# A two-layer graph attention kernel on one core: the two transfers of each attention row move from SyncE's queue to ScalarE's

## The reference

```python
def gat(h, adj, W, a):                  # one layer, per graph
    Wh = h @ W
    e = (Wh @ a_left)[:, None] + (Wh @ a_right)[None, :]
    e = where(e > 0, e, 0.2 * e)
    attention = softmax(where(adj > 0, e, very_negative), axis=-1)
    return attention @ Wh

h = maximum(layernorm(x), 0)
x = x + elu(gat(h, adj, W0, a0))
h = maximum(layernorm(x), 0)
x = x + gat(h, adj, W1, a1)
```

## Time and profile before

| what | us |
|---|---|
| median of three timed runs (lowest, highest) | 301.15 (300.55, 301.64) |
| the profiled execution, its own time | 300.98 |
| its span (first to last instruction) | 299.0 |
| TensorE busy in it | 289.5 (97%) |
| VectorE busy | 259.1 (87%) |
| ScalarE busy | 190.8 (64%) |
| transfers of q1, SyncE's queue, as a share of 16 DMA engines' span | 73.3% |
| mean granted TensorE clock, of 1 | 0.989 |

### The profile page before, as it was taken

One profiled execution on the slowest core, in us unless ns is written; L12 is line 12 of the kernel. 1 busy time (PEld: TensorE's weight loads), 2 busy tenths in 40 slices (PEclk: granted clock), 3 DMA queues, 4 the chain that ended last, 5 costly groups with the idle time before them and its releaser, 6 DMA issues.

```text
span 299.0 us, 6658 instructions
## 1 busy us (share of the span) xinstructions
PE 289.5 (97%) x2541; PEld 287.7 (96%) x2541; DVE 259.1 (87%) x538; ACT 190.8 (64%) x489; POOL 82.5 (28%) x157
## 2 busy tenths in 40 slices
PE   7999997599999999999999999999999999999996
PEld 7999997599999999999999999999999999999996
DVE  4798794599898989989898998979798879879896
ACT  3387681768594968769496877748574764754410
POOL 2721704002507052340706134240705124000000
PEclk9999999599999999999999999999999999999999
DMA  7999996939779593949769395985959789682012
GB/s 231 415 406 410 407 404 183 412 156 375 301 271 411 161 412 144 405 173 347 287 200 414 78 390 195 343 352 192 384 196 360 284 293 398 179 328 110 35 72 70
DMA packets 26383, 83.59 MB, mean 280 GB/s; under 512 B 4976, under 2 KB 6128, under 8 KB 26352
## 3 DMA queue, kind: packets, MB, share of 16 engines
q1 hardware_dynamic: 25776, 82.78, 73.3%
q10 hardware_dynamic: 576, 0.39, 0.4%
HBM read 78.91 MB, written 4.25 MB: 278 GB/s over the span
## 4 chain that ended last, share of the span: by engine, by line
PE 92%; DMA 4%; ACT 1%; DVE 0%; issue 0%; POOL 0%; POOLq 0%
PE acc L905 70%; PE prj L844 10%; PE tp L783 5%; DMA r_rows<-sqr 3%; PE acc L920 2%; PE acc L775 2%; DMA row_by_node<-r_rows 1%; PE prj L847 1%; ACT row_r L417 1%; PE prj L816 1%; PE tp L852 1%; PE prj L920 1%; PE prj L905 1%; PE acc L825 1%; ACT wh L389 0%; ACT hT L375 0%
## 5 line engine op out<-in xcount | busy, mean ns | idle before, releaser
L905 PE MATMUL acc<-wh,pbuf 128*128 128x129 f32 x1968 | 227.8, 275 | 0.2
L905 PEld LDWEIGHTS acc<-wh,pbuf 128*128 128x128 f32 x1968 | 224.2, 192 | 0.5 <-ACT wh L359 0.3
L660 DVE SCALAR_TENSOR_TENSOR pbuf<-row_r,sqr,adj_sb 128x1024 f32<-128x1024 f32 x126 | 156.3, 1276 | 12.3 <-ACT row_r L417 12.3
L424 ACT ACTIVATE accs<-accs,rec 128x128 f32<-128x128 f32 x120 | 36.7, 389 | 43.7 <-DVE rec L679 43.7
L268 POOL TENSOR_TENSOR mean<-stats 128x8 f32<-128x8 f32 x14 | 11.6, 830 | 148.2 <-DVE stats L548 147.0
L369 ACT ACTIVATE xn<-x_sb,shift,rstd 128x128 f32<-128x128 f32 x120 | 47.7, 479 | 0.0
L417 ACT ACTIVATE row_r<-row_by_node 128x1024 f32<-128x1024 f32 x14 | 29.5, 2105 | 17.4 <-DMA row_by_node<-r_rows 17.2
L844 PE MATMUL prj<-w_ext,hT 128*128 128x130 f32 x240 | 31.1, 286 | 5.1 <-ACT hT L375 5.1
L844 PEld LDWEIGHTS prj<-w_ext,hT 128*128 128x128 f32 x240 | 29.7, 201 | 5.2 <-ACT hT L375 5.2
L389 ACT ACTIVATE wh<-prj,wh 128x128 f32<-128x128 f32 x120 | 32.8, 364 | 0.0
L297 POOL TENSOR_TENSOR rstd<-vareps,neg_half 128x8 f32<-128x8 f32 x15 | 26.0, 1731 | 6.8 <-DVE vareps L567 5.7
(11 more groups left out here) (102 smaller groups left out, 177.5 us busy)
## 6 DMA issues: line engine op xcount, KB each, us to landing
adj_sb<-in_adj SPq DMA_DIRECT2D x128, 512.0 KB, 9.2
row_by_node<-r_rows SPq DMA_DIRECT2D x14, 512.0 KB, 4.4
x_sb<-in_x SPq DMA_DIRECT2D x7, 512.0 KB, 5.3
out_x<-x_sb SPq DMA_DIRECT2D x7, 512.0 KB, 8.8
x_sb<-in_x ACTq DMA_DIRECT2D x1, 256.0 KB, 3.5
x_sb<-in_x SPq DMA_DIRECT2D x1, 256.0 KB, 3.3
r_rows<-sqr SPq DMA_DIRECT2D x14, 4.0 KB, 2.2
out_x<-x_sb SPq DMA_DIRECT2D x1, 192.0 KB, 1.9
```

Source lines behind the costliest of these rows:

```text
L424: op = nc.scalar.activation(hp[:, t, :], hp[:, t, :], ACT.Copy, scale=rec[:, t:t + 1])
L660: nc.vector.scalar_tensor_tensor(pbuf[:, t, :], row_r[:, n % 2, :], sqr[:, n % 2, 0, t:t + 1], adj_at(n, t), ALU.max, ALU.min).then_inc(p_ ...
L905: mm = nc.tensor.matmul(sum_at(k, s), pbuf[:, t, i * P:(i + 1) * P], wh[:, n % 2, t, :], start=(t == 0 and s == 0 and k < NB), stop=(t == ...
```

## The change

`load_row` is gone from SyncE's program. Its two halves become `write_r` and `read_row` on ScalarE, with the same semaphores. `write_r(n+1)` stands right behind `exps(n+1)`. `read_row(n+1)` stands behind `elu_exp` in turns 1 to 8, and in the middle of `normalise` in later turns. SyncE's loop issues x, then all eight tiles of adjacency, then a store; the split of three and five tiles is gone. No arithmetic is changed.

```diff
-            def load_row(m):
-                k = loaded_rows(m)
-
-                line = r_rows.rearrange("t p -> (t p)")
-                sp.wait_ge(sqr_ready, m + 1)
-                sp.dma_start(line.rearrange("(p t) -> p t", t=T),
-                             sqr[:, m % 2, 2, :]).then_inc(r_written, 16)
-                sp.wait_ge(r_written, 16 * k)
-                if k > 1:
-                    sp.wait_ge(row_sorted, k - 1)
-                sp.dma_start(row_by_node[:, :], line.partition_broadcast(P)).then_inc(row_in, 16)
...
             for n in range(1, LAST):
-                loads = n + 2 <= LAST
-                if loads:
-                    for t in range(3):
-                        load_adj(n + 2, t)
-                load_row(n + 1)
                 if n + 4 < B:
                     load_x(n + 4)
-                if loads:
-                    for t in range(3, T):
+                if n + 2 <= LAST:
+                    for t in range(T):
                         load_adj(n + 2, t)
...
+            def write_r(m):
+
+                act.wait_ge(sqr_ready, m + 1)
+                nc.scalar.dma_start(r_rows.rearrange("t p -> (t p)").rearrange("(p t) -> p t", t=T),
+                                    sqr[:, m % 2, 2, :]).then_inc(r_written, 16)
+
+            def read_row(m):
+                k = loaded_rows(m)
+                act.wait_ge(r_written, 16 * k)
+                if k > 1:
+                    act.wait_ge(row_sorted, k - 1)
+                nc.scalar.dma_start(row_by_node[:, :],
+                                    r_rows.rearrange("t p -> (t p)").partition_broadcast(P)
+                                    ).then_inc(row_in, 16)
...
                 if n < LAST:
                     exps(n + 1)
+                    write_r(n + 1)
                     if elu:
                         elu_exp(n - 1)
+                        read_row(n + 1)
                     if n + 2 <= LAST:
-                        normalise(n + 2)
+                        normalise(n + 2, range(T // 2))
+                    if not elu:
+                        read_row(n + 1)
+                    if n + 2 <= LAST:
+                        normalise(n + 2, range(T // 2, T))
```

## The result

| what | before | after |
|---|---|---|
| median of the timed runs, us | 301.35 (300.55 to 301.64) | 320.02 (318.82 to 324.99) |
| ratio, 95% interval | | 1.0617 (1.0586 to 1.0648) |
| the profiled execution, us | 300.98 | 319.7 |
| its span, us | 299.0 | 317.9 |

A forecast was written before the change was run, and what follows sets the result against it. TensorE was taken to bound the kernel, outside one stall of 7.50 us. Less 2.0 for four full-queue stages and 0.4 for later turns, 5.1 us gained takes 300.98 to 295.9, as median 296.0; range 293.3 to 303.0.

The forecast's parts named there:

- The bound and the one stall: TensorE, busy 97% of the span, bounds the kernel; only the stage 2 row's late landing, 50.49 to 61.90, loses 7.50 us.
- The budget of 8.05 us for w + r: Write landing (w) plus read landing (r) of a stage's row may take 8.05 us; each stage pays the excess.
- The write on ScalarE's queue beside a full one: Write of r beside SyncE's full queue: w = 3.3 us, bounds 2.2 and 4.3.
- The read: Row read on ScalarE's queue beside SyncE's transfers: r = 5.05 us, bounds 4.4 and 5.7.
- How many turns: Four stages meet a full SyncE queue at 0.5 us each, 2.0 us; turns 5 to 8 cost 0.1 each, 0.4.
- ScalarE's own time: ScalarE's issuing and waiting stay covered while w is under 3.4 or so: nothing; otherwise up to 0.7 us a turn.
- my signs of being wrong: ScalarE issues over 0.9 us, a write over 5 us, TensorE gaps ahead of its transposes, or gaps in the second layer.
- The clock: TensorE's lower clock after the stage 2 stall: all 2.45 us regained, unless half a microsecond's gap lowers it.
- rival 2: Row transfers: contention at its upper bound, 1.95 us over in each of four stages, 301 us (298 to 302); chance 0.15.
- Rival 4: Write of r still waits out the adjacency, landing after 8.6 us or later in three stages: 310 or more; chance 0.05.
- Rival 3: ScalarE's issues are held by SyncE's full queue, up to 1.43 us instead of 0.33: say 304 us; chance 0.15.

## Why the prediction was wrong, point by point

- **The bound and the one stall**: right. 7.50 us were there to be had, and a kernel without that stall has 293.62.
- **The budget of 8.05 us for w + r**: right. In the changed kernel turn 4, at 8.3, has a gap of 0.34 us, and no turn of the first layer over it is without one. In the second layer, where the sort stands behind all of the scaling, turns 12 and 13 had sums of 8.7 and 8.4 and no gap: there the budget is larger.
- **The write on ScalarE's queue beside a full one**: mis-sized. I took 3.3, with 4.3 as the upper bound, from a weight load at 2 us. It was 5.6 and 6.2. At 2 us SyncE's queue had only begun to fill; the row that I leaned on did not show the case. Nor was the queue empty in the earlier trace rows: two transfers were in flight when that write was issued.
- **The read**: the step that failed. I took 5.05, at most 5.7, on the idea that a transfer shares the engines half and half with the other queue for its own length. It took 6.3 to 7.9 in all eight turns. The kernels with both transfers on ScalarE's queue show three cases: 3.5 to 3.7 with no burst (5.1 once), 5.2 to 6.3 with a burst that starts within 0.4 us of the read, 7.3 to 9.2 with one that starts 3 us and more ahead. My 5.05 comes near the second case only. What the sum left out is the wait ahead of the first byte: with full traffic ahead it is 3.5 us instead of 1.0. Also, what I called alone, 3.8 to 4.6, was in 13 of 14 turns a read with the next tiles issued right behind it on the same queue; alone it is 3.5 to 3.8.
- **How many turns**: this follows from the same step. I counted four turns with a full queue and put 0.1 us on turns 5 to 8, since w = 2.2 and r at most 5.7 kept them under 8.05. But there adjacency is issued tile by tile as masks end, always with two transfers in flight when the read is issued, and it took 7.3 to 7.9. Those four turns have 8.0 of the 20.4 us that were over, where I had 0.4; turns 1 to 4 have 12.4, where I had 2.0. A queue does not have to be full for this.
- **ScalarE's own time**: partly wrong. Its issues took 0.33 us as before. But I covered its stand on the write only up to w = 3.4 or so; with 5.6 and 6.2 xn came late for the transposes, 1.75 and 2.33 us in turns 1 and 2. That was one of my signs of being wrong. In the second layer and the last turn it cost nothing, as forecast.
- **The clock**: I said half a microsecond would not lower it, which held. I had no gaps of 2 us in mind. In three places the projection or the transposes ran slower after gaps of 2.2 to 2.3 us (a projection of 3.25 and of 3.51 us); after other gaps of the same length, and after one of 2.89, it ran in 2.05. That 2.05 is itself 0.26 more than the 1.79 of a projection without a gap, which my sum left out too.
- **The rivals**: rival 2, contention at its upper bound, was the mechanism, at more than twice its price in all and in eight turns instead of four; I had 301 for it. Rival 4 (the write waits out the adjacency) had a write of more than 5 us as its sign, and that sign came, but not the rival: the first write takes 5.4 to 5.6 us in the seven kernels that issue it from ScalarE into the first loads, whether 7 or 13 transfers of SyncE's are in flight, and in the changed kernel the last of these lands 11 us after it. Rival 3 (issue held) did not occur (the changed kernel, SyncE's queue and then ScalarE's):

```profile
29.55 10.18 SPq L208 DMA_DIRECT2D adj_sb<-in_adj  x8
...
38.43 0.34 ACTq L398 DMA_DIRECT2D r_rows<-sqr  x1
```

ScalarE's issue took 0.34 us while SyncE was in the middle of a run of eight that took 10.18 us, 1.27 each. So the rule of the Trainium skill that I had set beside rival 3 (Perfetto Trace Analysis, DMA Instruction — HWDGE (DVE, Sync): the generator is locked by one issuer) made no wait here that the profile shows. The rule of the Trainium skill, DMA: Bandwidth & Descriptors, Queues, rings and completion order, that engines take turns between the queues packet by packet, does not give the time of the read: worked out from it, my estimate was 5.7 us. The shares of the two queues come nearer to it only once the row flows. The first read of the changed kernel shows it, the 3.5 us from its issue on and then the rest, by queue as above:

```profile
q1 hardware_dynamic: 380, 1.39, 100.2%
...
q1 hardware_dynamic: 274, 1.00, 67.0%
q10 hardware_dynamic: 144, 0.52, 35.3%
```

That is the case of a full queue. In turns 5 to 7 it is less clear. These reads take 7.8 to 7.9 us while less than the full rate is moved, 302 GB/s in turn 5 where it is 407 in turn 1, though the engines count as busy for 0.88 of the time:

```profile
44.02:51.25 7.23, 5.48 (x50) 1.00 1.02 407
...
124.98:132.88 7.90, 7.90 (x73) 1.00 0.88 302
```

(stretch, length and busy time of TensorE, granted clock, DMA share, GB/s). What makes a read wait for its first byte behind traffic that is already flowing, and what takes it so long at 302 GB/s, no run here tells. The order of arrival decides by how much; the single source row has no part in what traffic adds.

## What to carry to other kernels

A wait at the head of an in-order transfer queue can be a useful dam: it kept bulk loads out of the way of a small, urgent round trip, and taking it away for "more overlap" cost seven times what the faster queue gained. Before giving a latency-bound transfer its own queue, ask what will be in flight when it starts, in every turn and not only in the one that stalls. If there is slack in bandwidth, put the urgent transfer first in each turn and a fixed number of bulk transfers behind it, so few that they drain before the next one.

## What was not expected of the hardware

- A 512 KB read takes 3.5 to 3.8 us alone, 5.2 to 6.3 when the other queue's burst starts within 0.4 us of it, and 7.3 to 9.2 when that burst started 3 us and more before it. In the last case its first byte moves 3.4 us and more after the issue instead of 1.0.
- A 4 KB write takes 1.4 us, over and over, with nothing in flight, 2 to 4 us at the tail of a burst, 3.5 to 4.5 when a burst starts with it, and 5.4 to 6.3 with 5 to 13 transfers of the other queue in flight, though none of them is ahead on its own queue.
- Two or three bulk transfers in flight, with 302 GB/s moved in all against 407 to 410 at full, are enough to slow the read by 4 us.
